# ScalarE takes over part of the row fetching and VectorE the copies of transposed rows, in an unrolled program, in a recommendation tower with dot interaction

## What is computed

```python
e = jnp.stack([tbl_f[ids[:, f]] for f in range(32)], axis=1)     # 512 x 32 x 256, float32
iu, ju = jnp.triu_indices(32, k=1)
z = jnp.einsum('bnd,bmd->bnm', e, e)[:, iu, ju]                   # 512 x 496 dot products
h = jnp.concatenate([z, dense_ctx], axis=1)                       # 512 x 512
h = jnp.maximum(h @ W_top1 + b_top1, 0.0)                         # 512 x 512
h = jnp.maximum(h @ W_top2 + b_top2, 0.0)                         # 512 x 256
y = h @ W_top3                                                    # 512 x 1
```

## Time and profile before

| | before |
|---|---|
| median of three runs | 179.75 us |
| the profiled execution, its own time | 179.57 us |
| span in the profile | 177.8 us |
| mean granted TensorE clock | 0.99 |
| busy: TensorE / GpSimd / VectorE / ScalarE | 142.3 / 119.3 / 61.5 / 59.0 us |

### The profile page before, as it was taken

The page is one execution under the profiler, slowest core; times in us unless marked ns, Lnnn a source line. Parts: engine busy times, 40 slices in busy tenths (PEclk is TensorE's granted clock), DMA queues, the critical chain, the costliest instruction groups (busy, mean ns, idle before and its releaser), DMA issues.

```text
span 177.8 us, 3958 instructions
## 1 busy us (share of the span) xinstructions
PE 142.3 (80%) x1122; PEld 128.3 (72%) x1122; DVE 61.5 (35%) x185; ACT 59.0 (33%) x185; POOL 119.3 (67%) x131
## 2 busy tenths in 40 slices
PE   0387665797689999767689999767679999789995
PEld 0175554786569999646579999646579999678993
DVE  2101615045150255634140255534140255576202
ACT  2011415124150261533151162533151162565210
POOL 4777777777777777777777777777777777760000
PEclk9999999699999999999999999999999999999999
DMA  0356876533343333333333333333343333331000
GB/s 17 90 165 233 285 228 188 169 101 118 96 123 101 115 110 105 110 104 119 92 121 97 116 104 107 111 102 118 95 121 96 116 103 110 109 102 33 0 0 0
DMA packets 8801, 19.69 MB, mean 111 GB/s; under 512 B 2706, under 2 KB 3730, under 8 KB 8788
## 3 DMA queue, kind: packets, MB, share of 16 engines
q0 software_dynamic: 6000, 16.39, 31.0%
q10 hardware_dynamic: 1874, 2.69, 4.8%
q1 hardware_dynamic: 914, 0.46, 0.9%
HBM read 19.54 MB, written 0.00 MB: 110 GB/s over the span
## 4 chain that ended last, share of the span: by engine, by line
PE 51%; POOL 21%; DMA 14%; issue 9%; ACT 2%; DVE 1%; DVEq 0%; ACTq 0%
POOL rows L169 21%; PE gram_ps L191 18%; PE act_ps L239 12%; DMA rows<-tables,idx 10%; PE xt_ps L184 10%; PE dve_ps L239 4%; DMA w_sb<-w 3%; PE act_ps L250 2%; PE dve_ps L250 2%; PE act_ps L258 1%; PE xt_ps L234 1%; DMA ids_sb<-ids 1%; ACT xt L379 1%; DVE z L123 1%; ACT z L123 1%
## 5 line engine op out<-in xcount | busy, mean ns | idle before, releaser
L169 POOL DMA_INDIRECT rows<-tables,idx x125 | 118.6, 948 | 39.5 <-issue 29.6
L191 PE MATMUL gram_ps<-xt 128*128 128x128 f32 x512 | 71.4, 285 | 3.1 <-ACT xt L379 3.1
L184 PE MATMUL xt_ps<-ident,rows 128*128 128x128 f32 x250 | 47.5, 295 | 30.0 <-DMA rows<-tables,idx 26.5
L191 PEld LDWEIGHTS gram_ps<-xt 128*128 128x128 f32 x512 | 64.8, 199 | 4.8 <-ACT xt L379 4.0
L184 PEld LDWEIGHTS xt_ps<-ident,rows 128*128 128x128 f32 x250 | 29.0, 146 | 40.6 <-DMA rows<-tables,idx 29.2
L313 DVE COPY xt<-xt_ps 128x512 f32<-128x512 f32 x32 | 22.1, 692 | 83.8 <-PE xt_ps L184 83.5
L123 ACT COPY z<-gram_ps 32x64 f32 (+5 forms) x136 | 34.6, 254 | 36.1 <-PE gram_ps L191 34.7
L123 DVE COPY z<-gram_ps 32x64 f32 (+5 forms) x136 | 34.4, 253 | 6.4 <-PE gram_ps L191 4.7
L379 ACT COPY xt<-xt_ps 128x512 f32<-128x512 f32 x31 | 18.1, 584 | 54.1 <-PE xt_ps L184 53.9
L239 PE MATMUL act_ps<-z,w_sb 128*128 (+1 forms) x192 | 22.4, 277 | 0.3 <-DVE z L123 0.3
L239 PEld LDWEIGHTS act_ps<-z,w_sb 128*128 128x128 f32 x192 | 21.7, 192 | 0.9 <-issue 0.5
(11 more groups left out here) (18 smaller groups left out, 11.4 us busy)
## 6 DMA issues: line engine op xcount, KB each, us to landing
sp_rows<-tables SPq DMA_DIRECT2D x384, 1.0 KB
w_sb<-w ACTq DMA_DIRECT2D x8, 256.0 KB, 3.4
rows<-tables,idx POOLq DMA_INDIRECT x125, 2.8
w_sb<-w ACTq DMA_DIRECT2D x1, 512.0 KB, 5.0
ids_sb<-ids SPq DMA_DIRECT2D x1, 64.5 KB, 1.9
z<-dense ACTq DMA_DIRECT2D x1, 64.0 KB
sp_ids_sb<-sp_ids ACTq DMA_DIRECT2D x1, 3.0 KB
vec_sb<-vectors ACTq DMA_DIRECT2D x1, 4.0 KB, 1.7
```

Source lines behind the costliest of these rows:

```text
L169: pool.indirect_dma_start(rows[:, g % STEP, :], None, tables, bass.IndirectOffsetOnAxis(idx[:, g:g + 1], 0)).then_inc(rows_landed[g % STEP ...
L184: last = nc.tensor.transpose(xt_ps[:, bank, place, P * k:P * (k + 1)], x[:, P * k:P * (k + 1)], ident[:])
L191: last = nc.tensor.matmul(gram_ps[:, n // HALF, n % HALF, :], x, x, start=(k == 0), stop=(k == CHUNKS - 1))
```

## The change

Fetching: five groups instead of three are fetched row by row. SyncE takes groups 43 and 86 and 112 rows of group 123 (368 rows, in this order), ScalarE the other 16 rows of group 123, and groups 66 and 118 (272 rows, in this order, 5 after each pair's other work). GpSimd gathers the other 123 groups into the same 16 slots.

Copies: VectorE copies every pair. The 16 pieces of dots of an octet (8 groups) are split 12 to 4: VectorE makes 4 pieces after each of three following copies, ScalarE 2, 1 and 1. In the last octet both have 8 pieces as before. The last two groups change places: VectorE copies the half of group 126, ScalarE that of group 127.

Network: h1's parts go alternately to `act_ps` and `dve_ps`, one part after each of four pairs. Block b's h1 parts come after pairs 16b + 20, 21, 22 and 23, h2 after 16b + 25 and y after 16b + 27, for b = 0, 1, 2. ScalarE has the relu of parts 0 and 2, VectorE that of parts 1 and 3. y's two products are taken in reverse order. 17 spare transposes stand in the place of 18.

There are no hardware loops any more; ScalarE loads one part of the weights with each of the first 9 pairs, and TensorE waits for them only at the first block.

```diff
-SP_GROUPS = tuple(GROUPS - STEP + n for n in (2, 3, 13))
-SP_ROWS = len(SP_GROUPS) * P
-IDLE_PASSES = 18
+SP_GROUPS = (43, 86)
+ACT_GROUPS = (66, 118)
+SHARED_GROUP = 123
+SHARED_BY_SP = 112
+SINGLE_GROUPS = SP_GROUPS + (SHARED_GROUP,) + ACT_GROUPS
+LOAD = 32
+ACT_ROWS_A_PAIR = 5
+GATHERED = tuple(g for g in range(GROUPS) if g not in SINGLE_GROUPS)
+IDLE_PASSES = 17
+DVE_QUADS = (0, 1, 2)
+ACT_QUADS = (3,)
+DVE_SHARE = ((0, 4), (4, 8), (8, 12), (12, 12))
+ACT_SHARE = ((0, 2), (2, 3), (3, 4), (4, 4))
...
+        def fetch_rows(engine, kind, lo, hi):
+            _, starts = nc.values_load_multi_w_load_instructions(
+                row_at[:, lo:hi], engines=[kind], min_val=0, max_val=(tables.shape[0] - 1) * ROW_BYTES,
...
+            for n, start in enumerate(starts):
+                group, p = divmod(lo + n, P)
+                yield engine.dma_start(single_u8[p:p + 1, group, :], tables_u8[bass.ds(start, ROW_BYTES)]
+                                       ).then_inc(single_landed[group], 16)
...
             # TensorE
+            for pair in range(1, PAIRS - 1):
+                transpose_pair(pair)
+                gram_pair(pair - 1)
+                mlp_at(pair)
+            transpose_group(GROUPS - 2, 1, 0)
+            gram_pair(PAIRS - 2)
+            transpose_group(GROUPS - 1, 0, 0)
+            pe.wait_ge(xt_ready, PAIRS)
+            gram_group(GROUPS - 2, 1, 0)
+            pe.wait_ge(xt_act, 1)
+            gram_group(GROUPS - 1, 0, 0).then_inc(gram_done, 1)
...
             # VectorE
+            for pair in range(PAIRS - 1):
+                copy_pair(pair)
...
+                octet, at = divmod(pair - 1, OCTET_PAIRS)
+                if octet >= 1 and at < OCTET_PAIRS - 1:
+                    last = dots(OCTET * (octet - 1), OCTET, DVE_QUADS, DVE_SHARE[at])
+                    if at == OCTET_PAIRS - 2:
+                        last.then_inc(z_dve, 1)
+                mlp_at(pair)
+            dots(GROUPS - 2 * OCTET, OCTET, DVE_QUADS, DVE_SHARE[2]).then_inc(z_dve, 1)
+            octet = GROUPS - OCTET
+            dots(octet, OCTET // 2, (0, 1), (0, 4))
+            dve.wait_ge(transposed, GROUPS - 1)
+            nc.vector.tensor_copy(xt[:, 1, 0], xt_ps[:, 1, 0]).then_inc(xt_ready, 1)
+            dots(octet, OCTET // 2, (0, 1), (4, 8))
+            dots(octet + OCTET // 2, OCTET // 2, (0, 1), (0, 8)).then_inc(z_dve, 1)
...
             # ScalarE
+            for pair in range(PAIRS - 1):
+                load_weights(pair)
...
+                mlp_at(pair)
+                some_rows(ACT_ROWS_A_PAIR)
+            dots(GROUPS - 2 * OCTET, OCTET, ACT_QUADS, ACT_SHARE[2]).then_inc(z_act, 1)
+            octet = GROUPS - OCTET
+            dots(octet, OCTET // 2, (2, 3), (0, 4))
+            act.wait_ge(transposed, GROUPS)
+            nc.scalar.copy(xt[:, 0, 0], xt_ps[:, 0, 0]).then_inc(xt_act, 1)
+            dots(octet, OCTET // 2, (2, 3), (4, 8))
+            dots(octet + OCTET // 2, OCTET // 2, (2, 3), (0, 8)).then_inc(z_act, 1)
```

More of the change, by code:

```diff
@@ L109, in tower_kernel, with copy_dots, stage_of @@
         y_done = sem("y_done")
-        y_free = sem("y_free")
+        y_copied = sem("y_copied")
         y_stored = sem("y_stored")
         z_by_quad = z[:].rearrange("p s (g q) -> p q g s", q=QUADS)
[L115 to L125, removed]
-            return last
+        def copy_dots(copy, quads, first, count, part):
+            o, at = first // OCTET, first % OCTET
+            pieces = [(q, jq) for q in quads for jq in range(QUADS)][part[0]:part[1]]
+            for q, jq in pieces:
+                lo = 1 if jq == 0 else 0
+                j0 = FIELDS * q + SLOTS * jq
+                last = copy(
+                    z_by_quad[FIELDS * jq:FIELDS * (jq + 1), q, first:first + count, lo:SLOTS],
+                    gram_ps[FIELDS * q:FIELDS * (q + 1), o % 2, at:at + count, j0 + lo:j0 + SLOTS])
+            return last
+        def fetch_rows(engine, kind, lo, hi):
+            _, starts = nc.values_load_multi_w_load_instructions(
+                row_at[:, lo:hi], engines=[kind], min_val=0, max_val=(tables.shape[0] - 1) * ROW_BYTES,
+                skip_runtime_bounds_check_because="each DMA checks its own address against the table's end")
+            for n, start in enumerate(starts):
+                group, p = divmod(lo + n, P)
+                yield engine.dma_start(single_u8[p:p + 1, group, :], tables_u8[bass.ds(start, ROW_BYTES)]
+                                       ).then_inc(single_landed[group], 16)
+        def stage_of(pair, delay):
+            b, at = divmod(pair - delay - OCTET_PAIRS, BLOCK_PAIRS)
+            return b - 1 if at == 0 and 1 <= b < BLOCKS else None
         block = ctx.enter_context(nc.Block())
@@ L132, in _ @@
             sp.dma_start(ids_sb[:], ids).then_inc(ids_loaded, 16)
[L135 to L147, removed]
+            sp.wait_ge(row_at_ready, 1)
+            for lo in range(0, SP_ROWS, LOAD):
+                for _ in fetch_rows(sp, mybir.EngineType.SP, lo, min(lo + LOAD, SP_ROWS)):
+                    pass
+            sp.wait_ge(y_copied, BLOCKS)
             sp.dma_start(y.rearrange("b o -> o b"), y_row[:]).then_inc(y_stored, 16)
@@ L193, in gram_group, with transpose_pair @@
                 return last
-            def transpose_pair(s, p, last=False):
+            def transpose_pair(pair):
                 for place in range(2):
[L197 to L241, removed]
-                last.then_inc(h1_done, 1)
+                    transpose_group(2 * pair + place, pair % 2, place)
+            def gram_pair(pair):
+                octet = pair // OCTET_PAIRS
+                if pair % OCTET_PAIRS == 0 and octet >= 2:
+                    pe.wait_ge(z_dve, octet - 1)
+                    pe.wait_ge(z_act, octet - 1)
+                pe.wait_ge(xt_ready, pair + 1)
+                gram_group(2 * pair, pair % 2, 0)
+                gram_group(2 * pair + 1, pair % 2, 1).then_inc(gram_done, 1)
@@ new lines, in h1_part @@
+            def h1_part(b, m):
+                if m == 0 and b:
+                    pe.wait_ge(h2_act, b)
+                elif m == 1 and b:
+                    pe.wait_ge(y_copied, b)
+                elif m >= 2:
+                    pe.wait_ge(h1_dve if m % 2 else h1_act, 2 * b + 1)
+                for s in range(SLOTS):
+                    last = nc.tensor.matmul(h1_ps[m], w1_sb[:, s, P * m:P * (m + 1)],
+                                            z[:, s, BLOCK * b:BLOCK * (b + 1)],
+                                            start=(s == 0), stop=(s == SLOTS - 1))
+                last.then_inc(h1_done, 1)
@@ L244, in h2_all, with h1_first @@
+            def h1_first(b):
+                octets = (b + 1) * BLOCK_PAIRS // OCTET_PAIRS
+                pe.wait_ge(z_dve, octets)
+                pe.wait_ge(z_act, octets)
+                if b == 0:
+                    pe.wait_ge(dense_loaded, 16)
+                    pe.wait_ge(w1_loaded, 16 * SLOTS)
+                h1_part(b, 0)
             def h2_all(b):
+                if b == 0:
+                    pe.wait_ge(w2_loaded, 16)
+                pe.wait_ge(h1_act, 2 * b + 2)
                 for m in range(N2):
@@ L254, in y_all @@
             def y_all(b):
[L255 to L259, removed]
-                last.then_inc(y_done, 1)
[L262 to L268, removed]
-                    h1_part(col, range(N1 - 1))
-                return {1: first, 2: lambda: h1_part(col, [N1 - 1]),
-                        4: lambda: h2_all(b), 5: lambda: y_all(b)}
@@ L274, in _ @@
[L274 to L287 removed]
+                if b == 0:
+                    pe.wait_ge(vec_loaded, 16)
@@ new lines, in y_all, with mlp_at @@
+                pe.wait_ge(h2_dve, b + 1)
+                for m in reversed(range(N2)):
+                    if m == 0:
+                        pe.wait_ge(h2_act, b + 1)
+                    last = nc.tensor.matmul(y_ps, w3[:, m:m + 1], h2[:, m, :],
+                                            start=(m == N2 - 1), stop=(m == 0))
+                last.then_inc(y_done, 1)
+            def mlp_at(pair):
+                for stage, delay in ((h1_first, 0), (lambda b: h1_part(b, 1), 1), (lambda b: h1_part(b, 2), 2),
+                                     (lambda b: h1_part(b, 3), 3), (h2_all, 5), (y_all, 7)):
+                    b = stage_of(pair, delay)
+                    if b is not None:
+                        stage(b)
@@ L289, in _ @@
+            for _ in range(IDLE_PASSES):
+                nc.tensor.transpose(xt_ps[:, 1, 0, 0:P], ident[:], ident[:])
+            b = BLOCKS - 1
+            h1_first(b)
+            for m in range(1, N1):
+                h1_part(b, m)
+            h2_all(b)
+            y_all(b)
         @block.vector
@@ L342, in h1_relu, with dots @@
+            def dots(first, count, quads, part):
+                dve.wait_ge(gram_done, (first + count) // 2)
+                return copy_dots(nc.vector.tensor_copy, quads, first, count, part)
```

(66 more changed lines are left out.)

209 lines of the change are left out of this document (81 added, 128 removed).

## The result

The changed kernel takes 184.97 us (median of four runs, 184.44 to 185.81) beside 179.84 for the kernel before: ratio 1.0289, 95% interval 1.0273 to 1.0305. It is slower by 2.9%; 179.3 was forecast.

A forecast was written before the change was run, and what follows sets the result against it. It took GpSimd's gather rhythm to fix the last landing, then 4.4 us of closing work and 12 us of network and store. From 179.57, -0.49 + 0.14 = -0.35 gave 179.22, stated as 179.3; range 177.1 to 182.0.

The forecast's parts named there:

- Two gathers fewer: GpSimd's chain: 2.50 us off, last gather starting at 156.05 and landing at 158.9; the most this path can bring.
- SyncE's rows: SyncE's 368 row fetches: row 368 starts at 152.1, group 123 is there at 154.0, TensorE wants it at 155.4.
- rival C: SyncE comes too late, slowed while ScalarE issues DMAs: 0.0084 us more a row, 3.1 in all, 180.6 us; chance 0.20.
- ScalarE's rows: ScalarE's row fetches: 0.3225 us each, about 8 of an octet's 10 us; its late start of some 5 us is covered.
- group 105 ... start 131.04, landed 133.9: Third block's network start: the 103rd gather lands at 133.9, and TensorE runs late without waiting from pair 52.
- VectorE's queue: VectorE is the busy one from 151.35 us; last dots end at 165.3 against 165.77, so 0.5 of 2.5 us arrive.
- Rival E: TensorE's clock falls while it stands from about 160.0 to 162.3 us, slowing the network: about +4, 183 us; chance 0.03.
- Rival B: The closing part follows the last gather as before, so the whole step arrives: 177.2 us; chance 0.12.

The follow-up runs named there:

- e4: The changed kernel with ScalarE fetching 144 rows instead of 272, 3 a pair, and GpSimd gathering 124 groups: 179.58 us (ratio 0.9993).
- e1: The changed kernel with no rows fetched by ScalarE; GpSimd gathers 125 groups, SyncE fetches 384 rows: 181.17 us (ratio 1.0077).
- e6: The changed kernel, last but one octet's dots split 4 VectorE, 12 ScalarE, VectorE's half copy of group 126 right after pair 62's copy: 182.91 us.
- e11: The kernel of e1 with ScalarE also fetching 188 unused rows of 1 KB, 3 a pair: 181.60 us (ratio 1.0131).

## Why the prediction was wrong

*Two gathers fewer* was right: the last one starts at 156.33. *SyncE's rows* was right that SyncE is hardly slowed (row 368 at 151.8, duration 0.228 as before); rival C's slower SyncE did not come. *ScalarE's rows* was right: five take 1.54 us, the last starts at 144.5, and ScalarE has no part in the chain that ended last. The rows were costed as issue time alone, on the issuing engines.

**The step that failed** is "group 105 ... start 131.04, landed 133.9". It took the landing time of 2.84 us from a trace in which one engine carried SyncE's rows only, and carried it over to one with 1.8 times as many (2.5 a us from SyncE, 2.0 from ScalarE). That gather took 8.0 us. Rival C looked for contention of the two issuers; it was in the engine that their DMAs share with the gathers, and it hit the gathers, not the rows. The mean busy share of the DMA engines, 37% before, hid it: it is a mean over sixteen, and all single rows went to one of them.

From there the working holds with a shift. Third network: 140.37 instead of 135.04, +5.3. Last dots: 170.39 instead of 165.28, +5.1; in between, the queue of *VectorE's queue* ran as priced (TensorE's wait 2.38 us forecast as 2.3, the half copy at its place). Then the spare transposes add 1.25, and the first network part, at 1.93 us instead of 1.78, together with smaller things 0.2. The sum is 6.55: a span of 177.45 was forecast, 184.0 measured. e4 checks the rest: there group 105's gather starts as in the forecast, so the same working gives 179.3 without the lateness; the last dots end at 165.5 (165.28) and 179.58 was measured. In e1 that gather is one period later, which would make 180.5; 181.17 was measured, inside the 181 to 182.5 on record.

Rival E was given 0.03. Its wait came at the right place, and in the profiled run the clock did fall; the cost was 1.4 us there and not 4, since the clock was back at 2.4 GHz from 172 us on, and the low stretch fell on the spare transposes for the most part. Rival B's idea, that the closing part need not grow, needed e6's order to come true.

## What to carry to other kernels

Ask for each DMA how many of the 16 engines it uses, and add up the number of DMAs on the fullest one: here a 64-byte DMA delayed that engine as much as one of 1 KB, and every gather, which spreads over all engines, landed as late as its share on that one. A landing time from a trace holds for the load on that trace. When an engine is given work because it is idle on average, look at its last 10 us before the end: VectorE had room for all copies, but not in front of the last two.

## What the runs showed that I had not expected

The lateness does not grow without limit: in the changed kernel the sixteenth update comes at 5.6 us with 4.4 single rows a us (40 to 100 us) and at 6.9 with 4.6 (from 100 us on), and GpSimd is never stopped; with 3.7 rows a us (e11) it comes at 2.8 to 3.0. Less than one row a us thus decides over 4 us. Where between 3.7 and 4.4 the step lies, and how steep it is, no run shows. The same 1 KB costs its issuer 0.235 us as one piece and 0.546 as sixteen.
